# First stage of a fused transformer kernel: the message's transposes, their copy and the routing weights put elsewhere in the order of work

## What is computed

```python
q = (x @ Wq).reshape(B, L, H, d);  feat = elu(q) + 1          # B, L, D = 8, 512, 128, H = 8 heads
KV = einsum('nshd,nshv->nhdv', feat, q / L);  Z = 1 / (einsum('nlhd,nhd->nlh', feat, feat.sum(1)) + eps)
msg = einsum('nlhd,nhdv,nlh->nlhv', feat, KV, Z) * L
msg = msg.reshape(B, L, D) @ Wm
x = x + layernorm(msg, g1, b1) + layernorm(relu(msg @ W1) @ W2, g2, b2)
x = layernorm(x_in + x)
logits = x @ router_w.T                                        # then the best 8 of 64 experts and their weights
```

## Time and profile before

| | us |
|---|---|
| median of 3 runs | 648.25 |
| the profiled execution, time | 652.67 |
| its span, first to last instruction | 650.7 |
| steps 0 to 10 of the first stage | up to about 137 |
| steps 3, 4, 5 of it | 12.89, 12.88, 12.89 |
| search for the expert slots | about 137 to 168 |
| gathers, experts, scatters | about 168 to 260 |
| second layer | from about 260 |

### The profile page before, as it was taken

One profiled execution on the slowest core, in us unless ns is written; L12 is line 12 of the kernel. 1 busy time (PEld: TensorE's weight loads), 2 busy tenths in 40 slices (PEclk: granted clock), 3 DMA queues, 4 the chain that ended last, 5 costly groups with the idle time before them and its releaser, 6 DMA issues.

```text
span 650.7 us, 10440 instructions
## 1 busy us (share of the span) xinstructions
PE 562.6 (86%) x3231; PEld 459.8 (71%) x3231; DVE 462.1 (71%) x1568; ACT 305.8 (47%) x825; POOL 427.9 (66%) x471
## 2 busy tenths in 40 slices
PE   5889888899238877999899999999999999999993
PEld 4678777855226655787687887878878788788762
DVE  1577877789949423576677879778787787886873
ACT  3667756449201111225364736636456365463440
POOL 5453422319574576538887988979979799753673
PEclk9999989799555555579999999999999999999998
DMA  4688455789320121142330030300302100000000
GB/s 130 170 229 316 186 218 196 313 255 233 80 73 28 47 61 50 37 170 99 127 131 2 8 138 9 135 4 10 138 9 93 46 9 9 2 17 0 10 8 17
DMA packets 47225, 62.04 MB, mean 95 GB/s; under 512 B 13026, under 2 KB 39873, under 8 KB 46146
## 3 DMA queue, kind: packets, MB, share of 16 engines
q1 hardware_dynamic: 44610, 56.15, 26.8%
q0 software_dynamic: 2560, 5.23, 2.8%
HBM read 35.16 MB, written 24.13 MB: 91 GB/s over the span
## 4 chain that ended last, share of the span: by engine, by line
PE 59%; DVE 19%; issue 6%; ACT 6%; POOL 3%; DMA 3%; another core or an unknown queue 2%; SPq 1%; POOLq 0%; DVEq 0%; ACTq 0%
PE pair L1446 8%; PE pair L1448 8%; PE pair L1447 8%; PE pair L1779 5%; DVE c_g L1247 2%; PE pair L602 2%; PE pair L628 2%; PE pair L1558 2%; DVE cand L1975 2%; PE pair L1494 2%; PE pair L1789 2%; PE pair L1568 2%; PE pair L555 2%; POOL c_acc L959 2%
## 5 line engine op out<-in xcount | busy, mean ns | idle before, releaser
L959 POOL TENSOR_TENSOR c_acc<-c_acc,c_g 128x512 f32<-128x512 f32 x112 | 144.6, 1291 | 37.6 <-DVE c_g L1247 30.0
L1095 ACT ACTIVATE c_sg<-pair 128x256 f32<-128x256 f32 x256 | 95.3, 385 | 93.3 <-PE pair L1448 90.4
L1247 DVE SCALAR_TENSOR_TENSOR c_g<-pair,c_comb,c_sg 128x256 f32<-128x256 f32 x224 | 100.4, 478 | 27.0 <-ACT c_sg L1095 22.7
L1446 PE MATMUL pair<-c_w_hi,c_x3h 128*128 128x512 f32 x256 | 108.9, 426 | 12.2 <-DVE c_g L1247 11.3
L1448 PE MATMUL pair<-c_w_hi,c_x3l 128*128 128x512 f32 x256 | 101.0, 395 | 0.0
L1447 PE MATMUL pair<-c_w_lo,c_x3h 128*128 128x512 f32 x256 | 100.7, 393 | 0.0
L1446 PEld LDWEIGHTS pair<-c_w_hi,c_x3h 128*128 128x128 f32 x256 | 48.2, 188 | 23.5 <-DVE c_g L1247 14.2
L1448 PEld LDWEIGHTS pair<-c_w_hi,c_x3l 128*128 128x128 f32 x256 | 48.0, 188 | 11.2
L1447 PEld LDWEIGHTS pair<-c_w_lo,c_x3h 128*128 128x128 f32 x256 | 48.3, 189 | 8.0
L1857 POOL DMA_INDIRECT routed_rows<-x1T_all,dest_row x32 | 31.7, 992 | 28.9 <-DVE x1T_all L1769 21.2
L1852 POOL DMA_INDIRECT rows_all<-token_rows,tok_row x32 | 31.3, 978 | 14.8 <-issue 9.4
(11 more groups left out here) (374 smaller groups left out, 1489.3 us busy)
## 6 DMA issues: line engine op xcount, KB each, us to landing
routed_rows<-rows_all SPq DMA_DIRECT2D x8, 2048.0 KB
c_c<-routed_rows SPq DMA_DIRECT2D x7, 2048.0 KB, 7.8
token_rows<-a_xw SPq DMA_DIRECT2D x8, 384.0 KB, 2.8
a_x<-in_L_attn_x SPq DMA_DIRECT2D x8, 256.0 KB, 3.0
base_all<-a_xw SPq DMA_DIRECT2D x8, 256.0 KB, 3.5
c_c<-routed_rows SPq DMA_DIRECT2D x4, 512.0 KB, 5.2
out<-c_outb SPq DMA_DIRECT2D x16, 128.0 KB, 1.8
wgu_late<-in_L_ffn_w_gate SPq DMA_DIRECT2D x4, 480.0 KB, 7.7
```

The lines of the kernel that those rows point to most:

```text
L959: g.tensor_tensor(acc, acc, b["g"][:, (2 * uf + i) % 4, :, :], ALU.add).then_inc(s["acc"], 1)
L1095: a_.activation(b[f"sg{q % 2}"][:, x, :], self.pair[q % 2][:, x, H1:2 * H1], SIG).then_inc(s["sig"], 1)
L1247: v.scalar_tensor_tensor(out=dst, in0=self.pair[q % 2][:, x, 0:H1], scalar=b[f"comb{uf}"][:, j * E1 + e:j * E1 + e + 1], in1=b[f"sg{q % 2} ...
L1446: t.matmul(dst, w_hi, x_hi, start=start, stop=False)
```

## The change

In the steps in which q of the next sequence is made ahead (k = 0 to 5), PE transposes the message into bank 1, right behind q and behind three unread products, and ahead of x1's transposes; ACT copies it (`copy_msgT`) ahead of x1's copy, and only the first half of `read_q` (`negate_q`) stays ahead of it, while the copy of q (`keep_q`) goes behind x1's copy. The six unread products ahead of x1's transposes are gone in all steps but the last sequence's, which keeps its 20. In all steps the two halves of `hT` change banks: the first goes to bank 6 and no longer waits for the logits' copy, the second to bank 5 and waits. On DVE the routing weights go ahead of `z` and `msg`.

```diff
         def read_q(n):
+            negate_q(n)
+            keep_q(n)
+
+        def negate_q(n):
             act.wait_ge(s["q_mm"], n + 1)
             if n:
                 act.wait_ge(s["feat_sb"], n)
             a.activation(b["e"][:, :], bank[2][:, :], ACT.Relu, scale=-1.0).then_inc(s["negq"], 1)
+
+        def keep_q(n):
             if n:
                 act.wait_ge(s["kv_mm"], n)
...
+        def copy_msgT(n):
+            act.wait_ge(s["msgT_mm"], n + 1)
+            if n:
+                act.wait_ge(s["m2_mm"], n)
+            a.copy(b["msgT"][:, :], bank[1 if self.ahead(n + 1) else 0][:, :]).then_inc(s["msgT_sb"], 1)
...
-                a.activation(b["hT"][:, 0, :], bank[5][:, :], ACT.Relu).then_inc(s["hT_sb"], 1)
+                a.activation(b["hT"][:, 0, :], bank[6][:, :], ACT.Relu).then_inc(s["hT_sb"], 1)
                 act.wait_ge(s["hT_mm"], 2 * n + 2)
-                a.activation(b["hT"][:, 1, :], bank[6][:, :], ACT.Relu).then_inc(s["hT_sb"], 1)
+                a.activation(b["hT"][:, 1, :], bank[5][:, :], ACT.Relu).then_inc(s["hT_sb"], 1)
...
             if self.ahead(k + 1):
-                read_q(k + 1)
+                negate_q(k + 1)
+                copy_msgT(k)
...
-            n = k
-            if n < self.N:
-                act.wait_ge(s["msgT_mm"], n + 1)
-                if n:
-                    act.wait_ge(s["m2_mm"], n)
-                a.copy(b["msgT"][:, :], bank[0][:, :]).then_inc(s["msgT_sb"], 1)
+            if k < self.N and not self.ahead(k + 1):
+                copy_msgT(k)
             if k + 1 < self.N:
-                if not self.ahead(k + 1):
+                if self.ahead(k + 1):
+                    keep_q(k + 1)
+                else:
                     read_q(k + 1)
                 exponential(k + 1)
...
+            if 0 <= m < self.N:
+                dve.wait_ge(s["pick"], 5 * m + 3)
+                v.tensor_reduce(b["esum"][:, :], ex, AX.X, ALU.add).then_inc(s["pick"], 1)
...
+                v.tensor_tensor(b[f"xw{m % 2}"][:, :, D:ROW], ex, bcast_last(b["esum"][:, :], E0), ALU.mult).then_inc(s["w_sb"], 1)
             n = k
             if n < self.N:
                 num = pair[3][:, :, 0:2 * (D + H0)].rearrange("p b (t c) -> p b t c", c=D + H0)
...
-                if n >= 2:
-                    pe.wait_ge(s["lg_sb"], n - 1)
                 for h in range(2):
-                    t.matmul(bank[5 + h][:, :], b["WmW1"][:, h * D:(h + 1) * D], b["msgT"][:, :], start=True, stop=True).then_inc(s["hT_mm"], 1)
+                    if h and n >= 2:
+                        pe.wait_ge(s["lg_sb"], n - 1)
+                    t.matmul(bank[6 - h][:, :], b["WmW1"][:, h * D:(h + 1) * D], b["msgT"][:, :], start=True, stop=True).then_inc(s["hT_mm"], 1)
...
                 if self.ahead(k + 1):
                     q_products(k + 1)
+                    unread(3, bank[1])
+                    pe.wait_ge(s["msg_sb"], n + 1)
+                    transposes(bank[1], tile("msg")).then_inc(s["msgT_mm"], 1)
             n = k - 2
             if 0 <= n < self.N:
-                unread(20 if n == self.N - 1 else 6, bank[0])
+                if n:
+                    pe.wait_ge(s["x1T_kept"], n)
+                if n == self.N - 1:
+                    unread(20, bank[0])
                 pe.wait_ge(s["x1_sb"], n + 1)
                 transposes(bank[0], lambda j: b[f"xw{n % 2}"][:, j, 0:D]).then_inc(s["x1T_mm"], 1)
...
             n = k
-            if n < self.N:
+            if n < self.N and not self.ahead(k + 1):
                 if n >= 2:
                     pe.wait_ge(s["x1T_kept"], n - 1)
                 pe.wait_ge(s["msg_sb"], n + 1)
```

More of the change, by code:

```diff
@@ L491, in dve @@
                 v.tensor_tensor(by_half(ex), by_half(ex), mask, ALU.mult).then_inc(s["pick"], 1)
+            if 0 <= m < self.N:
+                dve.wait_ge(s["pick"], 5 * m + 3)
+                v.tensor_reduce(b["esum"][:, :], ex, AX.X, ALU.add).then_inc(s["pick"], 1)
+                dve.wait_ge(s["pick"], 5 * m + 4)
+                v.reciprocal(b["esum"][:, :], b["esum"][:, :]).then_inc(s["pick"], 1)
+                dve.wait_ge(s["pick"], 5 * m + 5)
+                if m >= 2:
+                    dve.wait_ge(self.xw_stored[m % 2], 32 * (m // 2))
+                v.tensor_tensor(b[f"xw{m % 2}"][:, :, D:ROW], ex, bcast_last(b["esum"][:, :], E0), ALU.mult).then_inc(s["w_sb"], 1)
             n = k
@@ L506, in dve @@
                 ins.then_inc(s["msg_sb"], 1)
[L507 to L515, removed]
             n = k - 1
```

## The result

| | before | after |
|---|---|---|
| median, same chip, four runs each | 648.34 us | 640.07 us (638.84 to 640.55) |
| ratio, 95% interval | | 0.9853 [0.9818, 0.9888] |
| the profiled execution | 652.67 | 640.13 |
| its span | 650.7 | 638.2 |
| start of `hT` in steps 1 to 8 | 19.35, 29.50, 43.87, 56.76, 69.64, 82.53, 99.51, 111.79 | 19.49, 29.65, 42.20, 54.66, 66.22, 77.75, 91.28, 103.38 |

The slot search starts 8.57 us sooner, as much as the medians gain. The profiled spans differ by 12.5, because the gathers and experts of the profile of before also took 3.4 longer; that execution lies 4.3 above the median of before, so I put those 3.4 down to it and not to the change.

A forecast was written before the change was run, and what follows sets the result against it. PE was taken to bound the first stage, with two waits for copies in each step. Steps 2 to 5 give 4.5, step 6 1.3, step 7 0.7: 6.5 us, from 648.25 to 641.7; whole range 637.5 to 646.5.

The forecast's parts named there:

- The order on PE: Steps 2 to 5: without msgT ahead of the logits and the logits' wait, hT starts 1.32 us sooner a step.
- DVE late by 0.4 in steps 3 and 5: DVE's list shifts by more than its idle, so z and msg come late, lengthening two steps by 0.4 us each.
- The load of x, 0.3 once: SP's load of x, at the slow end, lands after x's transposes are due, costing 0.3 us once.
- Step 6: Routing product ahead of z avoids POOL's r, 0.4 us; hT's first half no longer waits for the logits' copy, 0.9; together 1.3.
- Step 7: hT no longer waits 0.55 for the logits' copy; PE is free at 111.12 instead of 111.79, 0.7 us.
- rival (a): PE in steps 2 to 5: fewer pauses, so the fall at 82.53 may not come; 8.1 saved, 640.1 us; chance 0.17.
- Rival (b): Steps 6 to 8: PE idles where fillers stood, clock falls more often; 1.6 to 3.3 given back, 644.2 us; chance 0.20.
- Rival (c): DVE is the bound, the routing product being held until the power has ended; 645.0 us; chance 0.10.
- Rival (d): Experts' stage: PE's shorter program moves its fetches among the gathers, four more waits of 3.24; 6.5 slower, 654.7 us; chance 0.08.
- (e): The change does nothing, as hT is late for another reason, such as ACT behind with x1; 648 us; chance 0.04.

The follow-up runs named there:

- late_with_fill: Kernel before with only hT's banks and the routing weights' place changed: transposes late, six fillers kept; 626.32 us, ratio 0.9868.
- w1n_later: Changed kernel with the 2 MB load of c_w1n issued in SP's step 4 instead of step 1; 651.54 us, ratio 0.9972 to the kernel before.
- before_again: Kernel before, unchanged, profiled a second time; 651.68 us (one run).
- undo_weights: Changed kernel with the routing weights back behind the message on DVE; 644.71 us, ratio 0.9872 to the kernel before.
- no_fill3: Changed kernel without its three unread products behind q; 624.80 us, ratio 0.9850 to the kernel before.
- fill_back: Changed kernel with the six unread products back ahead of x1's transposes in steps 6, 7 and 8 only; 645.94 us, ratio 0.9883 to the kernel before.
- undo_banks: Changed kernel with hT's halves back in banks 5 and 6, both waiting for the logits' copy; 652.35 us, ratio 0.9965 to the kernel before.
- undo_transposes: Changed kernel with the message's transposes and copy late again, the three new fillers gone, the six still removed; 650.31 us, ratio 0.9932 to the kernel before.
- before_no_fill: Kernel before without its six unread products ahead of x1's transposes, the last sequence's kept; 638.19 us, ratio 1.0064.
- both_mended: Changed kernel with c_w1n's load in SP's step 4 and six fillers back in steps 6 to 8; 651.08 us, ratio 0.9976 to the kernel before.
- after_third: Changed kernel, unchanged, run on the third occasion; 645.56 us, ratio 0.9877 to the kernel before.

## Why the prediction was right, and where its terms were off

**The order on PE** (1.32 a step): right. Steps 4 and 5 went from 12.88 and 12.89 to 11.56 and 11.53. By late_with_fill it divides into 0.86 for banks and weights (12.89 to 12.03) and 0.50 for the transposes (12.03 to 11.53).

**DVE late by 0.4 in steps 3 and 5**: wrong, it never happened: step 5 took 11.53, and w1n_later, which has no wait for x, ran step 3 in 11.56. The features did come at 1.37 of the step, as the step on r had it: in step 4 into 5, r starts at 64.23 and the features at 67.59, 3.36 later. That shift is 1.29. It lost 0.81 to the idle ahead of `kvs` and 0.08 to a list that ran in 3.25 from the features to `kvs` and not in 3.33; `kvs` was 0.40 late. Then the wait ahead of the masked exponentials absorbed 0.29, and not the 0.2 that I allowed for, and from there to `z` the weights took 1.46 where the old gap had 1.59. `z` begins 7.35 into the step, 0.02 sooner than before. Three margins, each read about a tenth too small, were the whole term, twice 0.4.

**The load of x, 0.3 once**: mis-sized, and left out of the sum. In step 3 PE waited 0.74 and the step was 0.9 longer. The six executions with early transposes and the load in its old place have 12.46, 12.50, 12.14, 11.91, 12.33 and 12.04 there, so the term is 0.35 to 0.94. So steps 2 to 5, forecast at 4 x 1.32 - 0.8 = 4.5, gave 4 x 1.32 - 0.9 + 0.5 = 4.9, less 0.15 lost ahead of them. The 0.5 is step 2, which went from 14.37 to 12.55, but was 13.89 in before_again: the wait of 0.30 for x in the first execution. That 4.5 and 4.8 lie so close is luck: the term of 0.8 that did not come and the 0.5 of step 2 make up for the 0.9 of the load.

**Step 6**: 1.3 forecast for the order, 1.34 measured, of which undo_weights has 0.37 for the routing product (0.4). **Step 7**: 0.7 forecast, 0.62 measured.

**The clock** is the step that the forecast had wrong, though its range holds the result. I held rival (a), the clock that holds, at 0.17 and the forecast at "as before", because no row told why the fall came in step 6 and not in step 5. That question was the wrong one. The second execution of before has it in step 5, so the position is not a property of the kernel; the number of falls follows the order of the work more closely. Two executions of before have one `hT` each at half clock in steps 3 to 6, six of the changed order (after three times, undo_weights, no_fill3, fill_back) and late_with_fill have none there, undo_banks has two, and undo_transposes and before_no_fill have four each. w1n_later and both_mended, of the changed order too, have one each, behind their stall. That the changed order keeps the clock is thus shown by counts, most of them from one execution of a program, and not by a cause. The 1.65 of step 6 is the difference between forecast and result: 6.5 + 1.6 = 8.1, against 8.3. The rows that could have told it were there: `hT` stood behind waits of 0.68 and 0.72 in every step, and the change takes the second away.

What makes the clock fall no run shows. They show a direction for fillers taken out with nothing useful in their place: late_with_fill without its fillers is undo_transposes, and `hT` in steps 3 to 6 went from 1.98 to 3.51 to 3.65; before without them is before_no_fill, where four `hT` took 3.28 to 3.75 and not one.

**Rival (b)**, more falls because of the missing fillers in steps 6 to 8: right on the risk, not on the result. In step 8 the 40 passes ran at half clock for most of their 6.24 us and before them the logits took 1.97, but before had both already (1.97 at 120.57, then 6.96 for the 40 passes), so against that execution nothing was lost. Against before_again, where they took 1.32 and 6.14, something was: from `hT` of step 8 to the search it is 25.25 in before, 23.89 in before_again and 25.09 to 25.11 in the three of the changed kernel. The fall at q in after_third, in step 6 where the fillers are gone too, may be of this kind, 1.06 us in one execution of three.

**Rival (c)**, DVE as the bound: it did not come. The weights ended ahead of `z`, and `z` was not late. DVE has 0.6 us left in a step of 11.53, so it is likely the next bound. That the features do not hang on the weights is shown by undo_weights, whose steps 4 and 5 are 11.53 too. Its product took 1.40 beside r in step 6, as 1.39 in the earlier trace rows, and 0.42 in the changed kernel, ahead of r. The 645.0 of this rival takes the product to be held until the power has ended, and no run shows that: in undo_weights the products at 53.12, 64.65 and 76.19 started while the powers of 51.81, 63.34 and 74.88 (1.64 each) ran, and took 0.43, 0.43 and 0.42.

**Rival (d)**, the experts' stage: from first gather to last scatter it took 104.65 before and 101.23 after; it ends at 276.74 in the profile of before, not at about 260 as the table of the time before has it. On the second occasion it took 86.45 in the changed kernel, 86.09 in no_fill3, 86.10 in late_with_fill and 86.11 in before_no_fill, with programs of PE of different lengths, so there it did not depend on them; on the other occasions it lies between 101.2 and 106.6, too widely to tell. The long wait of an unknown queue is still there, in the chain of waits of the changed kernel:

```profile
178.01 5.36 another core or an unknown queue
```

What it is stays open. **(e)**, nothing: refuted.

The point on which the study turned is not one of the prediction's numbers: taking the fillers out with the transposes left late puts the search 5.5 us later (135.28 against 129.83 in late_with_fill), and with the transposes early it costs nothing in steps 2 to 5. The change works because the two were done together.

## What to carry to other kernels

When a part of an ordered list is moved, count the pauses that are left ahead of the next long product, not only what they add to the critical path: they may cost the product its full clock, here 1.6 us. One pause of 0.7 cost none of the steps 3 to 6 their clock, 0.94 and 0.79 all four, and pairs between them (0.59 and 0.72, 0.68 and 0.72, 0.73 and 0.55) none, one or two. Before fillers are removed, look at what stands where they stood: in this stage taking them out alone was slower by 0.6%, and once the next useful work was moved there it was free. A term that rests on slack in a second engine wants every wait in that engine's list added up to a tenth of a microsecond, and a large load on a queue is weighed by what is issued behind it (here a store that took 5.92 us to issue and not 0.36).

## What was not expected of the hardware

- Which step falls to half clock differs between two executions of the same program (82.53 with 3.59, or 69.22 with 3.31), while the number of `hT` at half clock in steps 3 to 6 was one in both. Elsewhere the number is not fixed either: of three executions of the changed kernel one fell around q of step 6.
- `hT` falls with no idle time right ahead of it: in undo_transposes it ran for 3.51 behind 1.45 us of work without a wait, with waits of 0.79 and, before that, 0.94 further back.
- The issue behind a 2 MB load on SyncE's queue took 5.92 us (6.39 in both_mended); the other seven issues of that line took 0.36 to 0.46.
- The kernel before took 653.3, 633.2 and 652.7 us on the three occasions. For the changed kernel nearly all of it lies in one stage: its first two profiles are 14.0 apart (640.13 and 626.17), and from the first gather to the last scatter 14.8 (101.23 and 86.45), while the slot search starts at 128.47 and 128.90.
